# One transformer layer on one core: new orders of work on all engines, y's zeros from GpSimd, and the feed-forward's hidden tiles loaded back with one transfer each

## The reference

```python
x = x + layernorm(attention(layernorm(x), w_qkv, w_dense))
x = x + layernorm(ffn(layernorm(x), w1, w3, w2))          # w's are given with block scales
# attention: 8 groups, 4 query heads each share a key head and a value head, head size 128
qkv = q @ w_qkv.T; scores = qh . kh / sqrt(128), causal mask; probs = softmax(scores)
out = (probs . vh) @ w_dense.T
# ffn: act_quant scales each token's block of 128 columns by amax/448 + 1e-12
g = linear(x, w1); u = linear(x, w3); y = linear(silu(g) * u, w2)     # 512 -> 1792 -> 512
```

## Time and profile before

| what | us |
|---|---|
| median of three runs | 1110.0 |
| the profiled execution | 1110.88 |
| its span in the profile | 1109.0 |
| PE busy in it | 1089.4 |
| DVE busy | 863.2 |
| POOL busy | 763.5 |
| ACT busy | 678.9 |

### The profile page before, as it was taken

How to read it: one execution, slowest core, us unless ns; L and a number is a source line. 1 busy time by engine, 2 the same in 40 slices (tenths; PEclk the granted TensorE clock), 3 DMA queues, 4 the chain that set the end, 5 groups by cost and what they waited for, 6 DMA issues and landing times.

```text
span 1109.0 us, 16605 instructions
## 1 busy us (share of the span) xinstructions
PE 1089.4 (98%) x5126; PEld 908.0 (82%) x5126; DVE 863.2 (78%) x1736; ACT 678.9 (61%) x1329; POOL 763.5 (69%) x756
## 2 busy tenths in 40 slices
PE   9999999999999999999999999999999899999997
PEld 7888888788888888888888888888887678888876
DVE  5645566658899899989999999997687965666667
ACT  6532233428889788888788897985677432223243
POOL 7854347537769969879798799778855755666633
PEclk9999999999999999999999999999999999999999
DMA  6454564445899898897998989984210133433322
GB/s 231 124 181 152 175 224 145 137 136 200 306 300 355 289 325 322 303 344 278 331 348 273 332 303 333 343 274 153 76 58 1 42 113 117 121 107 90 114 63 100
DMA packets 163536, 227.86 MB, mean 205 GB/s; under 512 B 37760, under 2 KB 126464, under 8 KB 158592
## 3 DMA queue, kind: packets, MB, share of 16 engines
q1 hardware_dynamic: 163456, 226.88, 61.0%
HBM read 130.50 MB, written 96.34 MB: 205 GB/s over the span
## 4 chain that ended last, share of the span: by engine, by line
PE 85%; DVE 6%; DMA 2%; ACT 2%; POOL 2%; issue 1%; SPq 0%; POOLq 0%; DVEq 0%; ACTq 0%
PE psS L1622 23%; PE psOY L1793 15%; PE psOY L1622 14%; PE psT L1622 14%; PE psOY L1808 13%; PE psT L1667 2%; PE psOY L1667 2%; PE psT L1774 2%; DMA squares_long<-p_scr_long 1%; DVE y L1409 1%; DVE squares_long L1351 1%; DMA p_scr_short<-probs_short 1%; DVE pT_lo L1264 1%; DMA p_scr_long<-probs_long 1%; ACT probs_long L1043 1%
## 5 line engine op out<-in xcount | busy, mean ns | idle before, releaser
L1043 ACT ACTIVATE probs_long<-probs_long,negmax 128x896 f32<-128x896 f32 (+9 forms) x124 | 122.2, 987 | 7.0 <-DVE negmax L1332 6.7
L685 POOL TENSOR_TENSOR pT_lo<-squares_long,pT_hi 128x896 fp32r<-128x896 f32 (+3 forms) x47 | 108.0, 2308 | 25.9 <-ACT pT_hi L1038 25.7
L813 POOL TENSOR_SCALAR hidden<-mask,hr,hs 128x128 f32<-128x128 f32 x112 | 49.4, 452 | 88.8 <-DVE hr L1429 88.8
L746 POOL TENSOR_SCALAR probs_short<-probs_short,rsum 128x256 f32<-128x256 f32 (+9 forms) x128 | 76.5, 610 | 46.4 <-DVE rsum L1339 46.2
L1808 PE MATMUL psOY<-wd_hi,oT_hi 128*128 128x512 f32 x256 | 103.5, 404 | 2.2 <-DVE oT_lo L1264 2.0
L1351 DVE STREAM_TRANSPOSE squares_long<-squares_long 128x1792 f32<-128x1792 f32 (+3 forms) x54 | 101.5, 1881 | 2.8 <-DMA squares_long<-p_scr_long 2.8
L1808 PE MATMUL psOY<-wd_hi,oT_lo 128*128 128x512 f32 x256 | 100.2, 391 | 0.0
L1808 PE MATMUL psOY<-wd_lo,oT_hi 128*128 128x512 f32 x256 | 100.1, 391 | 0.0
L1622 PE MATMUL psS<-kT_hi,qT_hi 128*128 128x512 f32 (+5 forms) x280 | 98.2, 351 | 1.4 <-DVE negmax L1332 0.7
L746 POOL TENSOR_SCALAR probs_long<-probs_long,rsum 128x896 f32<-128x896 f32 (+9 forms) x70 | 74.9, 1072 | 33.8 <-DVE rsum L1339 33.7
L1622 PE MATMUL psS<-kT_lo,qT_hi 128*128 128x512 f32 (+5 forms) x280 | 96.4, 344 | 0.0
(11 more groups left out here) (216 smaller groups left out, 3383.4 us busy)
## 6 DMA issues: line engine op xcount, KB each, us to landing
q_raw<-q_scr SPq DMA_DIRECT2D x64, 256.0 KB, 5.0
p_scr_long<-probs_long SPq DMA_DIRECT2D x14, 896.0 KB, 6.5
squares_long<-p_scr_long SPq DMA_DIRECT2D x14, 896.0 KB, 7.2
p_scr_long<-probs_long SPq DMA_DIRECT2D x12, 1024.0 KB, 5.6
squares_long<-p_scr_long SPq DMA_DIRECT2D x12, 1024.0 KB, 7.5
p_scr_long<-probs_long SPq DMA_DIRECT2D x14, 768.0 KB, 5.6
squares_long<-p_scr_long SPq DMA_DIRECT2D x14, 768.0 KB, 4.5
raw<-in_w_qk SPq DMA_DIRECT2D x10, 1024.0 KB, 6.3
```

The lines of the kernel that those rows point to most:

```text
L685: return nc.gpsimd.tensor_tensor(dst, source, hi.bitcast(F32), ALU.subtract)
L746: nc.gpsimd.tensor_scalar(row, row, rsum[:, column(t, u)], 1.0, ALU.mult, ALU.mult).then_inc(p_ready[lane(t)], 1)
L813: last = nc.gpsimd.tensor_scalar(to, columns_of(h_sb[:, m % 2, b * P:(b + 1) * P], to), hr[:, m % 2, b:b + 1], hs[:, m % 2, b:b + 1], ALU. ...
L1043: nc.scalar.activation(row, row, ACT.Exp, bias=negmax[:, column(t, u)], scale=-1.0, accum_out=lsum[:, column(t, u)]).then_inc(e_done[lane( ...
```

## The change

All five strings are new, of the same items in the same order within a kind; POOL has four new items Z n, which zero the four tiles of `y`, and DVE's memsets are gone. DVE waits for all four once, ahead of the feed-forward's loop. Of the strings, first and last lines stand here; the lines between differ in the same manner, by neighbours changing places. In items, PE's end is

```diff
-                  "w": each("up_1", PIECES)}
+                  "w": each("up_1", PIECES), "v": [("Z", n) for n in range(NT - LAG, NT)]}
...
-    SP_WEAVE = ("qqwkqqwqoqoiqpioqjoqiipqoojqiipopqjqojpiiopkqojjqiipoojqqiipwojoqqiippoqjojqpiioqpkoiqjijopoqqjiiwpoojiq"
...
-    PE_WEAVE = ("psppspssvvvvppssypspyspypvpvpspspssvvpvvpyvbbbbvssvvssyyyyvbbbyyysysbssbvvvbvvvvssyyyvyvbbsvsvybvyvyvyvb"
...
-             "ypypypvppvvvvppyyxyyvxxgyxygyyxgxgggxdgxdgdd")
-    ACT_WEAVE = (
...
-             "neerkohnhqeoeeekeohhqeoqeeoppeppopppepppeeppeaqeceopipppjeqopepaepepceppiacppjieeoeepjpeqepopapepcpepipp"
-             "jaeopepcppippppeejaocppixxogxxajgcxagxgijctgixgjtxdtgtgddtd")
-    DVE_WEAVE = (
...
-             "olsloarsaorpspppsaoppsppsarppspcprsdsroppesppsfasrocppdsprpsacsppesdppsrfrsosesppfrascpoprpdspspacpeppsf"
-             "rdoppsppppsreacrppdoppexfaoxcxgdfgacxxxggedwfzgexfwgzwxzgwzgwz")
-    POOL_WEAVE = (
...
-             "ndqknqllrrmmmmqnnqllmmqmmnnrmmqlnmqmrqknlmmlmmndqkrrqnmmlmmlqnqndmmllmmnqqrmmnrmlmqnkmqnlmqlndmmknqrllnm"
-             "mmmqrrnllnnqdnlnqurnunnqnuuunynnnqanxnuqnnzyaxynnaxnnnnnqnyanxnynnaxnynnnaxwwygwgawgxygaxgwgwgg")
+    SP_WEAVE = ("qwqkqqwqqooiqpioqojiqipojoiqqipopqjoqjipiqokpqjojipioqjoiiqpwooqqjiippqqojjoiioppkqoijijoqpwoqjiiqpqoqoj"
...
+    PE_WEAVE = ("psppspssvvvvppssypspysppvyppssvsppvspyvpvvvbbvbbssvssvyyyyvbbssybyybsybbsvvvvvvvssvyyybyvbssbvyvyvbvyvyv"
...
+                "ypypypvpvpvvvppyyxyyvxgyyxyxggyxgxgdgxgxdgdd")
+    ACT_WEAVE = (
...
+                 "fkeqohnreehoekeweeqohhoeqeoppppoppeppepeaepppqeceeopipppjeeoppqaepeppcpipeapjceeioqppjeeepopapcppeipeppj"
+                 "eeoppaepppepecppaiopcpxioxgjxxjagxcgixgatcjgdixjtgxgdttgdtd")
+    DVE_WEAVE = (
...
+                 "olrsloasaoppppssraospppparscppsdpprssroppsseppfasorcsppppdspasrpsecrspdpsferosppfrascpsopdpppsrpeapcpsfs"
+                 "roppdpssppracrpppodppxaexecogfxgdxfxacgxgwdezfgexwfzgxwgzwzgwz")
+    POOL_WEAVE = (
...
+                  "ndqknllmmdmmrrqnqnllmmmmnqnqrmmrlqnqmmknlmmmmlqdnkqmmmnrrmllnqnqmmdrllmmnrmmqqnmmqlnkqnllqmmdnmmknqrllnm"
+                  "rmmmnqqnlldnnrqlrnnnzuunununqnyunannnxunnqyanxqynanxnnnnqnyaxnnnnyannnnxyaxwwygwgvawyxgagvxwggwgvvg")
...
-        h_scr = nc.dram_tensor("h_scr", [RING, P, CW], F32, kind="Internal").ap()
+        h_scr = nc.dram_tensor("h_scr", [RING, HG, P, CW // HG], F32, kind="Internal").ap()
         p_scr = [nc.dram_tensor(f"p_scr_{n}", [2, HG // 2, P * 2 * size], F32, kind="Internal").ap()
...
         wd_ready = sem("wd_ready")
-        eps_ready, down_step = sem("eps_ready"), sem("down_step")
+        eps_ready, down_step, y_zero = sem("eps_ready"), sem("down_step"), sem("y_zero")
         mean_y, var_y, rstd_y, off_y, yn_ready = (sem(n) for n in ("mean_y", "var_y", "rstd_y", "off_y", "yn_ready"))
...
             return tile if q < G // 2 else tile.rearrange("p (k s a) -> p k s a", a=HG, s=TURN_ROWS)
+
+        def by_tokens(turned):
+            return turned.rearrange("p (k q a) -> p k a q", k=CB, a=HG)
+
+        def in_tokens(block_):
+            return block_.rearrange("p (k a q) -> p k a q", k=CB, a=HG)
...
                 sp.wait_ge(h_ready, n + 1)
-                sp.dma_start(h_scr[m % RING], hidden[:, m % RING, :]).then_inc(h_out[m % 2], 16)
+                sp.dma_start(h_scr[m % RING].rearrange("c p x -> p c x"),
+                             hidden[:, m % RING, :].rearrange("p (c x) -> p c x", c=HG)).then_inc(h_out[m % 2], 16)
                 sp.wait_ge(h_out[m % 2], stored)
-                for c in range(HG):
-                    sp.dma_start(hidden[c * SPAN:(c + 1) * SPAN, slot, :].rearrange("q (a x) -> q a x", a=HG),
-                                 h_scr[slot, :, c * CW // HG:(c + 1) * CW // HG].rearrange("(a q) x -> q a x", a=HG)
-                                 ).then_inc(h_in[slot], 16)
+                sp.dma_start(hidden[:, slot, :], h_scr[slot].rearrange("c (q a) x -> (c q) (a x)", a=HG)
+                             ).then_inc(h_in[slot], 16)
...
                     quantise_hidden(args[0], args[0])
+                elif kind == "Z":
+                    pool.wait_ge(t_full, T_ATT + args[0] + 1)
+                    nc.gpsimd.memset(y[:, LAST[args[0]], :], 0.0).then_inc(y_zero, 1)
                 elif kind == "band":
...
                 act.wait_ge(t_full, T_ATT + i + 1)
-                nc.scalar.copy(tile_of(xn1T[0], LAST[i]),
-                               psT[:, i % 2, :].rearrange("p (a b) -> p a b", b=P)).then_inc(t_hi, 1)
+                by_fours = psT[:, i % 2, :].rearrange("p (k a q) -> p k q a", k=KT, a=HG)
+                nc.scalar.copy(tile_of(xn1T[0], LAST[i]).rearrange("p k (q a) -> p k q a", a=HG), by_fours).then_inc(t_hi, 1)
...
                 act.wait_ge(ht_full, n - (C * NT - LAST_TURNS) + 1)
-                nc.scalar.copy(hT[0][:, n % RING, :], psS[:, slot, BANK:BANK + CW]).then_inc(ht_hi, 1)
+                nc.scalar.copy(in_tokens(hT[0][:, n % RING, :]), by_tokens(psS[:, slot, BANK:BANK + CW])).then_inc(ht_hi, 1)
...
                 dve.wait_ge(t_hi, T_ATT + i + 1)
-                lo_part(lo, psT[:, i % 2, :].rearrange("p (a b) -> p a b", b=P), hi).then_inc(t_done, 1)
+                hi, lo = (t.rearrange("p k (q a) -> p k q a", a=HG) for t in (hi, lo))
+                lo_part(lo, psT[:, i % 2, :].rearrange("p (k a q) -> p k q a", k=KT, a=HG), hi).then_inc(t_done, 1)
...
                 dve.wait_ge(ht_hi, n + 1)
-                lo_part(hT[1][:, n % RING, :], psS[:, slot, BANK:BANK + CW], hT[0][:, n % RING, :]).then_inc(ht_done, 1)
+                hi, lo = (in_tokens(t[:, n % RING, :]) for t in hT)
+                lo_part(lo, by_tokens(psS[:, slot, BANK:BANK + CW]), hi).then_inc(ht_done, 1)
...
                     lo_of_xn1(*args)
-                    if args[0] >= NT - LAG:
-                        link(nc.vector.memset(y[:, LAST[args[0]], :], 0.0))
                 elif kind == "GU":
                 elif kind == "TT":
-                    turn_hidden(args[0], args[0], 16 * HG * (args[0] // RING + 1))
+                    turn_hidden(args[0], args[0], 16 * (args[0] // RING + 1))
                 elif kind == "TH":
...
             dve.wait_ge(d_done, NT - LAG)
+            dve.wait_ge(y_zero, LAG)
...
                 for m in range(2 * NT):
-                    feed_forward_step((2 * NT) * r + NT + m, NT + m, (16 * HG * 2 * NT // RING) * r + 16 * HG * ((NT + m - LAG + 1) // RING + 1))
+                    feed_forward_step((2 * NT) * r + NT + m, NT + m, (16 * 2 * NT // RING) * r + 16 * ((NT + m - LAG + 1) // RING + 1))
             for m in range(2 * NT):
                 n = (C - 2) * NT + m
-                feed_forward_step(n, n, 16 * HG * ((n - LAG + 1) // RING + 1), last=m - LAG - NT)
+                feed_forward_step(n, n, 16 * ((n - LAG + 1) // RING + 1), last=m - LAG - NT)
             lo_of_last(C * NT - 3, 1)
```

More of the change, by code:

```diff
@@ new lines, in sandwich_kernel @@
+    PE_WEAVE = ("psppspssvvvvppssypspysppvyppssvsppvspyvpvvvbbvbbssvssvyyyyvbbssybyybsybbsvvvvvvvssvyyybyvbssbvyvyvbvyvyv"
+                "ssbbybyyyvssbyvvyvvyyvssbbvvyyyyvvssyybyvvyvvvvvvsbsyybyyvbvvssyyyyvvvvvvvbsbsybbyyyvvbssyyvbyyvvvbvvbsb"
+                "syyyyvssvvvbyyvyyvssvvyyyyvvsbsbyyvvbvyvyvvvvbssyyyyvvvssbbyyyyvvvvvvvbbssybyyvyvbssbyyvybvvyvbvvbssyyyb"
+                "yvsbsyvvvyyvyvbssvvbyyyyvvssyyvbyyvvvvvvvbssybbyyyvvvssyyyyvvvvvvvbbssybbyyvyvssbyvybyvvvyvbvbssbyybyyvs"
+                "svvyvyvyyvbsbsvvybyyyvbvssyyyyvvvvvvvvbbssyvvyyyvssyyyyvvvvvvvbbsbybsyybyvvbssyyyvyvvvbvvbssyyyybvbssvyv"
+                "vvyyyvbssbyvvybyyvvssyybyyvvvvbbvvvvssvvyyyyvbbssyyyyvbvvvvvvsbbsyybyyvvssvbyyyvyvbvvvssbyyyyvssbbyvvvyv"
+                "yybvssvbyyvyyvvbssyyyyvvvvvvvvssyvvyyyvbsbsyyyyvvvvvvvssyyyvsysvssyyyvyvvvvvsyyyyvsvvyvyyvyvppssyppyyyvv"
+                "vvpspsyyppyyppsvpvspvvsvvvvppssyppyyyvvvssppsyypypypspsvpspsvvvvvvspspyyyvyvpspspsypypyypvpvpvvvvsppssyp"
+                "ypypypvpvpvvvppyyxyyvxgyyxyxggyxgxgdgxgxdgdd")
@@ new lines, in sandwich_kernel @@
+    DVE_WEAVE = ("psppspsrmsropspssppppsrpssrpsrppsrppabbbboisissrstrabbotslbsbsliirsutkarotblbssaiborubtisstrkabbsobliusb"
+                 "oalrsiustbrkboatsisabbolilusrsuaktbobrtlasbsibosrlisurtatobblkbbsiisaosrsutbbrktbaibollssauoirsukstraots"
+                 "bblsaolrbbissiturtuaosksblbaolbsibsiurtatrobbklsibsabousisrtbbrkatbioblssilauorussbktboratislsbbaoliurss"
+                 "ktrabuobtlsbsibaoilssratrutobbklbsbsiiaoutrssbbktarbiobsluislouarbssbtkobbriatisslaoulrsuskabbtortsslibb"
+                 "aoliursstrtabobkblsbisaiuorssktrbbatbibossulaolruibbsstraokbbtilissaouulsrsbbkbaibtiortssluaolsbrskbrbit"
+                 "atboslsabuibrosstirtbkabosislbluoaukrbbsstoratblssioaurlusiasktrotsbsbalbobslsriuaitrkotsslrssoausrksatt"
+                 "olrsloasaoppppssraospppparscppsdpprssroppsseppfasorcsppppdspasrpsecrspdpsferosppfrascpsopdpppsrpeapcpsfs"
+                 "roppdpssppracrpppodppxaexecogfxgdxfxacgxgwdezfgexwfzgxwgzwzgwz")
```

(4 more changed lines are left out.)

29 lines of the change are left out of this document (7 added, 22 removed).

## The result

The changed kernel takes 1103.72 us (median of 6 runs, 1101.17 to 1105.58), the one before 1110.22 in the same session (6 runs, 1109.66 to 1112.1): a ratio of 0.9939, 95% interval 0.9928 to 0.9950, so 5.6 to 8.0 us less. The forecast was 1105.4, the range 1101.0 to 1110.0. The sum was 1.7 us short, and its terms were less good than it: one gain did not come, one that was put at nothing came. The result lies about as near to rival 2's 1102.3 as to the forecast.

The account below looks back on a forecast made before the run. PE, busy 1089.4 of 1109.0 us, was taken as the bound, so only its holes could be won: -1.5 + 0 - 1.3 - 1.3 - 0.5 = -4.6, from 1110.0 to a median of 1105.4 us, range 1101.0 to 1110.0.

Parts of the forecast that it names:

- rival 2: Middle gains too: half its 3.52 us idle with 0.6 hidden goes, -2.4, clock stays up, -0.7: 1102.3; chance 0.20.
- last probabilities: Last attention tile: all four N63 ahead of root_x14 and root_y5 on POOL, ending PE's waits; -1.3 us (-1.3 to 0).
- start: First attention tiles: hole before Y2,0 (1.1 us) closes, 0.4 gained at DVE's maxima; -1.5 us (-2.2 to +0.5).
- middle: Long attention stretch of 535 us, 3.52 idle in some eight holes: new order no worse, 0 us (-2.0 to +1.5).
- count of covers: Attention, all 64 tiles: PE work between dependent items; PV-to-Y covers under 1.5 us short by 2.1 us before, 1.6 after.
- Hand-over: Between attention and feed-forward: old order loses 7.6 us, new 6.2 if the clock stays up; -1.3 us (-4.5 to +1.5).
- walk: Hand-over: new strings followed item by item from X0, waits at Y63,0, GU4, DN0, GU6, X7, GU7 summing to 6.2 us.
- slow clock: Hand-over, 889.5 to 893.6 us: PE's granted clock of 0.58 after holes costs 1.7 us; given 4 in 10 afterwards.
- rival 1: Hand-over no better: DVE pays 0.43 us for each xn1T_lo, +2.2, slow clock returns, +1.0: 1108.6; chance 0.17.
- The memsets: Hand-over: four of 485 ns move from DVE to POOL at cost 0; up to 1.9 us back if they delay DVE.
- Feed-forward: One load a tile instead of four ends its issue 1.4 us earlier, closing one PE hole; -0.5 us (-1.2 to +0.5).
- Rival 3: Attention exchange: loads behind one more 1024 KB transfer come late, 3.7 us per place, two places: +7.4, 1112.8; chance 0.11.

Follow-up runs that it names:

- loads alone: Kernel before with tokens by fours and one hidden load a tile instead of four, old orders, zeros on DVE: 1111.3 us, ratio 0.9999.
- zeros alone: Kernel before with y's four memsets moved from DVE to POOL, nothing else: 1111.63 us, ratio 1.0005.

## Why the prediction was right, and where not

The number came out near, partly by luck. What the last probabilities (1.3) and part of the start did not give, the middle gave, which the sum had at nothing.

**Start (forecast -1.5, found about -1).** The hole at Y2,0 closed, as counted. The step "nothing new is on the way" failed: I went through DVE's string for moved items and not through ScalarE's, where a cast that depends on a load had moved ahead of one more exponential, and Y0,0 paid 1.3 us. The 0.4 for the maxima of heads two apart is not sure either. The hole at S4,2 (0.3) closed in every kernel with the new start, but the one at S7,2, 0.4 in all with the old start, is nothing to 0.2 in four of nine traces and 0.9 to 2.1 in the other five. What decides between them was not looked for.

**Middle (forecast 0, found about -2.4, and -0.9 more in the last tiles).** This is the term that was mis-sized most, and rival 2, which had -2.4 for the middle, was right about it. The count of covers had seen only two kinds of pairs. In every kernel with the old order there, PE loses 0.76 and 0.50 us around S60,3 and Y58,0, just before 808; in the changed kernel nothing and 0.08. The trace of before names the wait, a score item for the maxima two heads earlier:

```profile
PE psS L1622 <- DVE negmax L1332: 0.5, 1, 0.5
```

Another 0.63 at S63,0 and 0.44 at Y61,0 are gone too. I had even noted S60,1 as the tightest cover, and counted it as unchanged. The rest of the middle cannot be put down to single places: under one and the same new order it loses between 8.3 and 13.9 us.

**Last probabilities (forecast -1.3, found 0).** GpSimd's scaling is in time (0.3 us of wait instead of 1.0), and PE then waits for the next chain that was nearly as late, O62's, now Y62's. PE in the changed kernel:

```profile
849.56 0.41 PE L1783 MATMUL psT<-ident,probs_short 128*128 128x128 f32 x2 [0.26 <-POOL probs_short L751]
850.83 0.50 PE L1817 MATMUL psOY<-wd_hi,oT_hi 128*128 128x512 f32 x1 [0.85 <-DVE oT_lo L1272]
```

The failed step is that I asked what stood behind POOL's items and not what is late next on PE. The old wait had been the cover of this one.

**Hand-over (forecast -1.3, found -2.2).** The walk was right in kind: DN1's wait went, X5's of 1.5 is gone in four of the eight traces with the new end and 0.6 in the other four (I had it gone), and DN0 (1.98), GU6 (1.64), GU4 (1.42, in four traces 0.5) came, against 1.9, 1.5 and 0.8. Three waits of the walk did not come: Y63,0 has 0.2 instead of 1.1, X7 nothing instead of 0.4 and GU7 0.1 instead of 0.5. So the walk's 6.2 for the new order is the mean that was measured, with errors that cancel.

What was mis-sized is the other side. The sum had 7.6 for the old order; its trace loses 8.9, and over five traces the old end loses 8.4. These are of two kinds. In three of them (the kernel before, and the kernels with new orders in the start only and in start and middle) the granted clock falls to a mean of 0.66 over 5 us behind the holes of X7 and DN1, mostly the lower level, and the stretch loses 8.9. In two (loads alone, zeros alone) it is 1.00 throughout, and it loses 7.3 and 7.9, with the same holes or longer ones. All eight with the new end and DN0 in its place have 1.00. So of the 2.2 us in the table roughly half is order, and half a slow clock that did not come back. xn1T_lo with its reads in steps took 684 ns against 678 before, so rival 1 fell:

```profile
L1272 DVE TENSOR_TENSOR xn1T_lo<-psT,xn1T_hi 128x512 fp32r<-128x512 f32 x7 | 4.8, 684 | 1.8 <-ACT xn1T_hi L1096 1.7
```

The Trainium skill's rule on lines of PSUM ("SBUF — State Buffer", section "Door 1: The DMA port swizzle"), which it states for matmuls, is not borne out by this read of DVE's.

The memsets were put at cost 0, and that step failed in part. In the changed kernel four products of scales lie beside a memset on GpSimd and take 0.86, 0.62, 0.79 and 0.60 us, where one alone takes 0.34: some 1.5 us in all of the 1.9 that DVE was spared. The prediction had named this as its bad case; the section after next shows the rows.

The slow clock, given 4 in 10, was rarer. A mean clock of 0.998 or less over the span was shown by 90 of 132 executions with the old end, and by 14 of 69 with the new one and DN0 in its place. In the traces it is worth 1.6 us (8.9 against 7.3), which agrees with the 1.7 of the earlier trace rows. In the timings it is worth less: of the kernel before, 39 executions at 0.997 or less had a median of 1110.9, 25 at 0.999 or more one of 1110.5. Why the two differ is open.

**Feed-forward (forecast -0.5, found -1.3, by timings about -1).** The mechanism was right (fewer issues, earlier load, waits of DVE shorter by a third). The size was taken from one hole of one trace that loses 1.2 us; the 1.3 rests on three traces that lose 2.5 to 3.2, and without them it is 0.6, so the forecast's size may have been right as well.

**Rival 3** is there as a pressure: DVE waited 2.1 us in the middle for the exchange before and 7.7 after, in ten places. In one execution of the changed kernel a single such wait of 3.7 us cost PE 2.5; in the other one that was profiled the longest is 1.6.

```profile
DVE squares_long L1359 <- DMA squares_long<-p_scr_long: 3.7, 1, 3.7
```

Rival 3 had priced such a place at 3.7 us and had two of them; this one cost 2.5.

## What to carry over

When a wait is removed, walk on to the next item of the bounding engine and ask how late its own chain is; here one wait had hidden another of the same size, and the gain was nil. When an order is changed, look in every engine's string for items that depend on a load and have moved forward. And where single executions scatter by several us, judge a stage by its loss in all the traces at hand, since here the same kernel, timed twice against the kernel before (on two chips), gained 4.0 us and 8.2, and most differences between variants were smaller.

## What the runs showed that was not expected

**VectorE is held up by some GpSimd instructions beside it, until they end.** The four products of scales (128x128, SBUF to SBUF) take 0.34 us each alone, and 0.35 to 0.39 beside GpSimd's scalings of 128x128. Beside an addition or a memset of 128x512 it is different. In the changed kernel the four of X5's tile took 2.46 us, and PE waited 1.2 us for what stood behind them (DVE, then POOL):

```profile
868.36 2.46 DVE L1417 TENSOR_SCALAR y<-y,qr,qs 128x128 f32<-128x128 f32 x4
870.74 0.68 DVE L1272 TENSOR_TENSOR xn1T_lo<-psT,xn1T_hi 128x512 fp32r<-128x512 f32 x1
```

```profile
868.93 0.52 POOL L955 MEMSET y<- 128x512 f32 x1
869.42 1.31 POOL L833 TENSOR_TENSOR x<-x,y 128x512 f32<-128x512 f32 x1
```

They took 0.39, 0.86, 0.62 and 1.30 us. The last started at 869.52, 0.1 us behind the addition on GpSimd, and took as long as that does; the 0.86 and the 0.62 lie beside the memset. When the changed kernel was profiled again, DVE stood 0.2 us earlier against GpSimd, and its last product (870.40, 0.63 us, beside the memset) began before the addition did:

```profile
869.63 1.41 DVE L1417 TENSOR_SCALAR y<-y,qr,qs 128x128 f32<-128x128 f32 x4
```

```profile
870.33 0.62 POOL L955 MEMSET y<- 128x512 f32 x1
870.92 1.28 POOL L833 TENSOR_TENSOR x<-x,y 128x512 f32<-128x512 f32 x1
```

The two levels of the hand-over with the new end go with this: in four traces with a product of 1.3 us for this tile PE loses 6.88 to 6.93 us there, in four without it 5.42 to 5.47. By these eight traces the same sequence of instructions is 1.4 us apart by how two engines happen to stand. It was seen, not tried by itself: no run took the addition away. The Trainium skill ("SBUF — State Buffer", section "SBUF: two separate sides") has the ports shared by the two engines as a lock that whichever starts first holds for its whole instruction. The addition's rows agree: the product that took 1.30 us started behind it. The memset's agree less well: the record of the product of 0.86 us starts 0.26 us ahead of the memset's and still ends behind it. My walk priced each product at a fixed 0.59, the mean of the earlier trace rows, which mixes 0.34 and 1.3. That accounts for GU4, off by 0.6 in the four traces with the long product; it was not followed through to the other waits that were off.
